# A second attention's inner loop: the order of turnings, mix and projection on TensorE, of copies and exponentials on ScalarE, and of maxima and addition on VectorE

## What is computed

```python
Q = query @ Wq.T + bq
K = key_value @ Wk.T + bk
V = key_value @ Wv.T + bv
# 16 heads of 32
scores = jnp.einsum('bhsd,bhtd->bhst', Q, K) * scale
attn = jax.nn.softmax(scores, axis=-1)
ctx = jnp.einsum('bhst,bhtd->bhsd', attn, V)
return ctx.transpose(0, 2, 1, 3).reshape(B, S, D_MODEL) @ Wo.T + bo
```

## Time and profile before

| what | value |
|---|---|
| median of 3 runs | 2813.0 us (2812.85 to 2819.16) |
| the profiled execution, its own time | 2817.72 us |
| its span, first to last instruction | 2816.0 us |
| TensorE (PE) busy | 2568.2 us, 91% of the span |
| VectorE (DVE) busy | 932.3 us, 33% |
| ScalarE (ACT) busy | 656.2 us, 23% |
| GpSimd (POOL) busy | 450.9 us, 16% |
| mean granted TensorE clock | 0.943 |

### The profile page before, as it was taken

How to read it: one execution, slowest core, us unless ns; L and a number is a source line. 1 busy time by engine, 2 the same in 40 slices (tenths; PEclk the granted TensorE clock), 3 DMA queues, 4 the chain that set the end, 5 groups by cost and what they waited for, 6 DMA issues and landing times. The chain is left out here.

```text
span 2816.0 us, 35498 instructions
## 1 busy us (share of the span) xinstructions
PE 2568.2 (91%) x10573; PEld 1460.8 (52%) x10574; DVE 932.3 (33%) x2320; ACT 656.2 (23%) x1467; POOL 450.9 (16%) x607
## 2 busy tenths in 40 slices
PE   7999999999899888888898999959699999969988
PEld 4343434345455465665654556435356556434476
DVE  5232323234311333413451222464122222431275
ACT  2343424253011024324320111021011111042131
POOL 6000000000311200000023111414311111510062
PEclk9999999998999989899889999959799999979989
DMA  9101010002265310000042665423244453451220
GB/s 373 41 1 34 0 34 0 0 0 66 84 205 187 104 34 5 12 16 5 1 151 89 191 201 177 116 68 119 73 145 159 139 158 118 130 192 70 79 92 27
DMA packets 150025, 260.39 MB, mean 92 GB/s; under 512 B 16022, under 2 KB 80638, under 8 KB 149421
## 3 DMA queue, kind: packets, MB, share of 16 engines
q1 hardware_dynamic: 115885, 182.52, 19.9%
q0 software_dynamic: 19072, 49.35, 6.2%
q10 hardware_dynamic: 14976, 27.27, 2.5%
HBM read 209.21 MB, written 49.88 MB: 92 GB/s over the span
## 5 line engine op out<-in xcount | busy, mean ns | idle before, releaser
L360 POOL DMA_INDIRECT slot_list<-token_ids,slots x64 | 62.0, 969 | 725.7 <-DVEq L546 706.9
L1457 DVE CUSTOM_DVE_ANT_0 l0a_p<-bank,xn 112x375 f32<-112x375 f32 x128 | 70.3, 549 | 299.4 <-PE bank L1302 236.3
L250 PE MATMUL bank<-ident,xn 112*128 112x112 f32 x256 | 60.1, 403 | 86.2 <-DVE xn L226 86.2
L917 PE MATMUL bank<-f2r_wd,f2b_hT 128*128 (+1 forms) x300 | 137.2, 593 | 1.4 <-DVE f2b_hT L1006 1.4
L898 PE MATMUL bank<-f2r_wg,f2b_xT 128*128 x400 | 128.8, 466 | 1.5 <-ACT f2b_xT L954 1.3
L1330 PE MATMUL bank<-l0a_vo,l0a_zT 128*112 128x512 f32 x256 | 127.7, 593 | 0.0
L898 PE MATMUL bank<-f2r_wu,f2b_xT 128*128 x400 | 126.5, 459 | 0.0
L1404 ACT ACTIVATE l0a_p<-l0a_p,l0a_low 112x375 f32<-112x375 f32 x128 | 77.8, 608 | 191.8 <-DVE l0a_low L1466 191.8
L1302 PE MATMUL bank<-l_krT,l0a_qrT 64*112 64x375 f32 x256 | 112.8, 521 | 0.0
L360 POOL DMA_INDIRECT slot_list<-token_ids,slots_in x32 | 31.2, 974 | 499.4 <-DVEq L546 490.2
L1301 PE MATMUL bank<-l_kvcT,xnT 128*112 128x375 f32 x256 | 103.0, 484 | 2.8 <-ACT xnT L1399 2.8
(11 more groups left out here) (374 smaller groups left out, 4655.7 us busy)
## 6 DMA issues: line engine op xcount, KB each, us to landing
slot_rows<-zeros SPq DMA_DIRECT2D x2, 7424.0 KB
slot_rows<-f2b_y ACTq DMA_DIRECT2D x50, 256.0 KB, 3.7
f1r_wg<-in_l_wg SPq DMA_DIRECT2D x16, 704.0 KB, 4.6
f1r_wu<-in_l_wu SPq DMA_DIRECT2D x16, 704.0 KB, 6.6
f2r_wg<-in_l_wg SPq DMA_DIRECT2D x16, 704.0 KB, 4.4
f2r_wu<-in_l_wu SPq DMA_DIRECT2D x16, 704.0 KB, 6.0
xn<-in_l_w_ffn SPq DMA_DIRECT2D x11, 768.0 KB, 4.3
l_raw<-in_l_w_ffn SPq DMA_DIRECT2D x11, 768.0 KB, 4.4
```

The lines of the kernel that those rows point to most:

```text
L250: mm = pe.transpose(s.bank[n % 4][:, k * TOK:(k + 1) * TOK], s.xn[:, n, k * 128:(k + 1) * 128], s.ident[0:TOK, 0:TOK])
L360: pool.indirect_dma_start(s.slot_list, bass.IndirectOffsetOnAxis(ap=slots[:, k, b:b + 1], axis=0), s.token_ids[:, b:b + 1], None, **bound) ...
L917: mm = pe.matmul(bank_y[v][:, :], hT[0:fn, v, c, :], wd[0:fn, bass.ds(at, 1), c, :].rearrange("p o f -> p (o f)"), start=(c == 0), stop=(c ...
L1457: dve.tensor_tensor_reduce(out=p[:, n % BUFS, :], in0=s.bank[n % 3][0:TOK, 0:T], in1=a.mask[:, b, :], scale=1.0, scalar=-3.0e38, op0=ALU.a ...
```

## The change

TensorE issues the four turnings of batch n - 1 one after another, then the mix of n - 2, then the projection of n - 3. ScalarE makes the four copies of batch n - 1, then the four exponentials of batch n. VectorE takes both maxima of n before it adds n - 4. No operation is added or taken away, and all waits stay as they are.

```diff
                     if 0 <= n - 1 < B:
-                        turn(g, n - 1, 0)
-                        turn(g, n - 1, 1)
+                        for j in range(GH):
+                            turn(g, n - 1, j)
                     if 0 <= n - 2 < B:
                         mix(g, n - 2)
-                    if 0 <= n - 1 < B:
-                        turn(g, n - 1, 2)
-                        turn(g, n - 1, 3)
                     if 0 <= n - 3 < B:
                         project(g, n - 3)
...
                 for n in range(B + 1):
-                    for pair in range(2):
+                    for j in range(GH):
                         if 0 <= n - 1:
-                            copy_turned(g, n - 1, 2 * pair)
-                            copy_turned(g, n - 1, 2 * pair + 1)
+                            copy_turned(g, n - 1, j)
+                    for j in range(GH):
                         if n < B:
-                            exponential(g, n, 2 * pair)
-                            exponential(g, n, 2 * pair + 1)
...
                 for n in range(B + 4):
-                    if 0 <= n - 4 < B:
-                        add(g, n - 4)
                     if n < B:
                         maximum(g, n, 0)
                         maximum(g, n, 1)
+                    if 0 <= n - 4 < B:
+                        add(g, n - 4)
                     if 0 <= n - 2 < B:
                         divide(g, n - 2)
```

More of the change, by code:

```diff
@@ L1674, in _ @@
                 for n in range(B + 1):
-                    for pair in range(2):
+                    for j in range(GH):
                         if 0 <= n - 1:
-                            copy_turned(g, n - 1, 2 * pair)
-                            copy_turned(g, n - 1, 2 * pair + 1)
+                            copy_turned(g, n - 1, j)
+                    for j in range(GH):
                         if n < B:
-                            exponential(g, n, 2 * pair)
-                            exponential(g, n, 2 * pair + 1)
+                            exponential(g, n, j)
         @block.vector
```

## The result

The changed kernel took 2820.8 us in the median of 8 runs (2817.9 to 2826.2), the kernel before 2813.8 (8 runs, 2807.1 to 2819.2). The ratio is 1.0027, 95% interval 1.0014 to 1.004: 7.6 us slower, between 4 and 11. That lies inside the stated range and just inside "same" (within 0.3%). The forecast was 2.9 us slower, so the sign was right and the size too small.

A forecast was written before the change was run, and what follows sets the result against it. Bound by a loop through TensorE and ScalarE: scores, mix, late turnings, two copies, two exponentials. Steady iterations -0.8, start-up -0.5, tails +4.2 gave +2.9 us, median 2815.9; range 2807 to 2825.

The forecast's parts named there:

- Steady iteration: Full-clock iterations behind the start-up of each loop: 5.28 instead of 5.34 us, 14 in all, 0.8 us saved.
- the semaphore's 0.05: Delay in us from copy 0's end (+1.90) to turning 2's start (+1.95), taken from the link between exponentials and scores.
- TensorE's own queue: TensorE's work in a steady iteration: projection ends at +4.84, 0.44 us before the next scores.
- the moved mix is hidden: Steady iteration: mix and sums, 1.29 us, moved behind all turnings, cost nothing within TensorE's 0.44 us of slack.
- The lower bound: Steady iterations if the wait for copy 0 costs nothing: TensorE's 4.84 us bounds, 6.2 us less, 2809.7.
- Start-up: Half-clock first iterations of each group: second +0.88, third 7.06, fourth 6.4 in two groups; 0.5 us saved together.
- Tail: Behind each group's last scores: division loses its cover, last mix at +9.33 instead of +8.28; +1.05 us each, +4.2 in all.
- The sum: Whole kernel: -0.8 - 0.5 + 4.2 = +2.9 us, so the median goes from 2813.0 to 2815.9.
- rival 1: Slower by the clock: two longer loops and one more low-clock stretch near each group's tail; +13.8 us, 2827; chance 0.18.
- Rival 2: Clock falls in every steady iteration, TensorE's work there 8.9 us; 51 us more, 2867; chance 0.02.
- Rival 3: Faster: ScalarE's queue closes up, start-ups get shorter low-clock stretches; 2805.1, needs copy 0 done by +1.57; chance 0.13.
- Rival 4: Two banks hold the turnings in pairs anyhow, losses and gains cancel; 2813; chance 0.07.

The follow-up runs named there:

- the split mix: Kernel before, with the mix's second half (the sums) moved behind turnings 2 and 3, old order behind the last scores; ratio 0.998 (0.9966 to 0.9994).

## Why the prediction was right, and where it was off

- **The bound.** That the steady period is a loop through TensorE and ScalarE, that turning 2 must wait for copy 0 in the new order, and that a division without cover appears in the tail: all shown, by the timeline after and by the three kernels that undo or isolate a part.
- **Steady iteration.** Forecast 0.06 less, measured 0.01 less (5.33 against 5.34). The term that failed is the semaphore's 0.05 taken for turning 2: with two waits ahead of it, 0.14. Without the second, turning 2 starts at the forecast +1.95 and the period is 5.26. The total over 14 iterations was 0.2 us instead of 0.8.
- **TensorE's own queue.** I gave 4.84 and 0.44 of slack; measured 5.19 (with ScalarE's old order), so 0.14 of slack. Three things were missing: the late turning (0.09), 0.08 more from turning 2 to the mix (0.83 where I had 0.74), and a projection that takes 1.04 to the next scores, not 0.86. The claim that the moved mix is hidden held, by less than I had said. The prediction calls the 4.84 TensorE's own work and uses it as what is left when the wait for copy 0 costs nothing, but turning 3's end at +2.69, from which it is added up, stands behind that wait. The lower bound (2809.7) was out of reach in this order.
- **Start-up.** +0.88 in the second iteration, 7.06 for the third: measured +0.8 to +1.0 in the first traces, +1.1 to +1.6 in the second (6.73 to 7.11 against 5.53 to 5.97), and 7.10. For the fourth, 6.4 was forecast in two groups, and 5.93 and 5.32 came. The steps held, but the low-clock stretches fall elsewhere in every execution. The first four iterations gained 1.6 us over the four groups in the first traces and 1.1 in the second, where 0.5 had been forecast; the whole loops 1.8 and 1.2, where 1.3 had been forecast.
- **Tail.** +1.05 in each group forecast, +1.40 measured, 5.6 us instead of 4.2. The mechanism was right, the size wrong by the same shifts: projection 0.17 later (+4.15), 0.09 for the second wait of turning 2, 0.08 more from turning 2 to the mix. The first turning came another 0.09 late, 0.95 behind the projection instead of 0.86, but its copy started 0.51 behind it and not 0.60, so that cost nothing: there the sum was right by luck.
- **VectorE.** Costed at nothing, and nothing it costs in the changed kernel. The addition ends at +3.84 and the projection comes at +4.15, 0.31 of room, all of which TensorE's new order gives; with the old one the projection is due at +3.70 and waits, as VectorE's order alone showed.
- **The sum.** 5.6 less 1.8 is 3.8, against the 2.9 forecast. The misses partly cancel: the steady iterations saved 0.6 less than forecast and the tails cost 1.4 more, but the start-up saved 1.1 more. The stage's stretch grew by 4.5 and 5.5 us in the two traces that each kernel has, laid in pairs (371.9 less 367.4, 372.2 less 366.7). The rest is in the gaps from one group's last scores to the next group's first. They grew by 2.86, 1.13 and 0.83 us in the first pair and by 1.54, 1.12 and 2.72 in the second, where the later mix alone gives 1.40. One gap in each pair pays for more time at the lower clock, in the next group's first queries projection, which is rival 1 in small. In the first gap of the first pair, before and after:

```profile
1102.09:1105.50 3.41, 3.41 (x6) 1.38 (x5) 0.00 (x0) 0.00 (x0) 0.00 (x0) 0.50 0.00 0
1105.50:1108.90 3.40, 3.40 (x11) 1.79 (x10) 0.00 (x0) 0.82 (x2) 0.00 (x0) 1.00 0.00 0
...
1101.26:1104.67 3.41, 2.75 (x4) 1.51 (x5) 0.00 (x0) 0.00 (x0) 0.00 (x0) 0.50 0.02 7
1104.67:1108.09 3.42, 3.42 (x6) 1.39 (x5) 0.00 (x0) 0.00 (x0) 0.00 (x0) 0.50 0.03 5
```

  Before, the clock was back at 1.00 at 1105.50, after the change at 1108.09. TensorE had stood idle for 2.8 us ahead of this projection before and 2.9 after, and for 2.5 to 3.1 us in all gaps of the four traces, so that pause does not tell the long gaps from the others, and no run shows why it was these. The measured 7.6 and 7.0 us have intervals that hold 5; what of the difference lies outside the stage, if any does, stays open.
- **Rival 2**, a clock that swings in every iteration, is out: all steady iterations of the changed kernel (the fifth to the seventh of each group) are 5.33 at a clock of 1.00. The rule of the Trainium skill cited in the prediction ("TensorE: Matmul & The Clock Gate", "A second HAM failure mode: psum-queue depth-cycling") says short pauses between bursts can bring the clock down. In this kernel pauses of 0.3 to 0.6 us did not; with ScalarE's order alone pauses of 1.5 us went with a fall in the seventh iteration of every group. **Rival 3** needed copy 0 to be done by +1.57; it ended at +1.90. **Rival 4** is nearest to the truth for the steady iterations alone.

## What to carry to other kernels

Reordering two engines that feed each other moved the waits here and did not remove them: chain both orders through by hand, and give the iterations without the usual cover (the first two, and those behind the last) their own sums, for here they decided the result. Where a step must wait for a buffer, put into the gap half of a block of work that is ready, as the split mix did (period 4.97 against 5.33), rather than move the whole block behind it. And before counting on an engine's slack, take the duration of an operation from where its new neighbour follows it, not from where an old one did.

## What was not expected of the hardware

- The projection takes 0.86 us to a turning right behind it in the kernel before (1407.52 to 1408.38), 0.95 with a mix ahead of it and a turning behind (1089.02 to 1089.97), and 1.04 with a mix ahead and scores in small 32-row tiles behind (1086.71 to 1087.75, TensorE's order alone). The first two differ by where the count starts: in the kernel before the projection's weights load from 1407.42, still under the matmul ahead, and from there it is 0.96; behind a mix, weights and matmul start together. Behind a mix, which works in 32-column tiles, the next weights of a whole tile come 0.17 late ("issue") in the timelines of all orders tried at full clock, 0.33 at the lower one. Why they do, no run took apart.
- A turning whose two waits are still to be worked off starts 0.14 us behind the end of the copy that it waits for, one with a single wait 0.05 (2.04 and 1.95 behind the scores, the copy ending at 1.90 both times). The extra instruction takes 51 ns in the trace. Where the turning was not late (the split mix with and without it), the period is 4.97 both ways.
